# Transformer block kernel: first GELU product in fp16 parts, six norm applications on ScalarE and the bias addition moved in the full iterations

## What is computed

```python
x = x + _layernorm(_L0_attn_ref(_layernorm(x), rotation, entangle))      # softmax attention, 16 heads of 16
x = x + _layernorm(_L0_ffn_ref(_layernorm(x), W_r, W_k, W_v, mu_r, mu_k))  # r * (relu(k)^2 @ W_v), token shift
x = x + _layernorm(_L1_attn_ref(_layernorm(x), ...))                     # linear attention, then a GELU layer
x = x + _layernorm(_L1_ffn_ref(_layernorm(x), w_gate, w_up, w_down))     # gated layer with integer weights
# inside _L1_attn_ref, after the linear attention:
x2 = _layernorm(x, g2, be2)
h = jax.nn.gelu(x2 @ w1.T + b1, approximate=False)     # w1: 1024 x 256
x = x + (h @ w2.T + b2)
```

## Time and profile before

| | |
|---|---|
| median of 3 runs | 3242.41 us (3236.66 to 3253.96) |
| profiled execution | 3249.45 us, its span in the trace 3247.7 us |
| TensorE busy | 2945.7 us (91%) |
| ScalarE busy | 2332.9 us (72%), mostly before 2040 us |
| VectorE busy | 1478.6 us (46%), mostly after 2040 us |
| GpSimd busy | 217.9 us (7%) |

### The profile page before, as it was taken

The page is one execution under the profiler, slowest core; times in us unless marked ns, Lnnn a source line. Parts: engine busy times, 40 slices in busy tenths (PEclk is TensorE's granted clock), DMA queues, the critical chain, the costliest instruction groups (busy, mean ns, idle before and its releaser), DMA issues. The chain is left out here.

```text
span 3247.7 us, 48002 instructions
## 1 busy us (share of the span) xinstructions
PE 2945.7 (91%) x18048; PEld 1178.1 (36%) x18048; DVE 1478.6 (46%) x3536; ACT 2332.9 (72%) x2586; POOL 217.9 (7%) x193
## 2 busy tenths in 40 slices
PE   2998998999999999998999999389999999999996
PEld 0221221222222222222222222256666666666654
DVE  6221220422331332232411311568888888866574
ACT  2999999999999999998999999223343333333332
POOL 0000000000000000000000000111111111111110
PEclk9999999999999999999999999699999999999998
DMA  3411111311210211111111110222122111111010
GB/s 114 141 39 35 62 38 33 99 37 41 82 37 33 91 58 41 62 35 60 63 43 35 37 41 22 65 64 66 53 71 72 58 58 58 46 52 53 26 46 21
DMA packets 125602, 177.70 MB, mean 55 GB/s; under 512 B 42248, under 2 KB 100616, under 8 KB 125128
## 3 DMA queue, kind: packets, MB, share of 16 engines
q1 hardware_dynamic: 122392, 172.53, 16.4%
q10 hardware_dynamic: 2992, 2.23, 0.2%
HBM read 107.62 MB, written 67.11 MB: 54 GB/s over the span
## 5 line engine op out<-in xcount | busy, mean ns | idle before, releaser
L714 ACT ACTIVATE probs<-ps 128x1024 f32<-128x1024 f32 x2048 | 1895.1, 1172 | 102.3 <-PE ps L456 101.2
L582 PE MATMUL ps<-probs,vals 128*32 128x512 f32 x8192 | 1099.8, 610 | 0.0
L456 PE MATMUL ps<-qT,kT 64*128 64x512 f16 x4096 | 730.9, 387 | 109.2 <-DMA kT<-split_dram 26.9
L456 PEld LDWEIGHTS ps<-qT,kT 64*128 64x128 f16 x4096 | 173.0, 93 | 1152.6 <-ACT probs L714 1029.1
L869 DVE COPY sums<-ps 128x512 f32<-128x512 f32 x64 | 44.2, 691 | 529.5 <-PE ps L582 529.5
L582 PEld LDWEIGHTS ps<-probs,vals 128*32 128x32 f32 x8192 | 162.7, 108 | 298.8 <-issue 235.1
L1304 PE MATMUL layers_ps<-yT,weight_mem 128*128 128x512 f32 x512 | 227.5, 595 | 10.8 <-ACT hT L1543 10.8
L1310 PE MATMUL layers_ps<-weight_mem,hT 128*128 128x256 f32 x1024 | 231.5, 380 | 0.0
L1570 ACT ACTIVATE gate<-layers_ps 128x512 f32<-128x512 f32 x96 | 57.3, 597 | 226.4 <-PE layers_ps L1458 226.4
L1310 PEld LDWEIGHTS layers_ps<-weight_mem,hT 128*128 128x128 f32 x1024 | 193.0, 190 | 29.8
L1458 PE MATMUL layers_ps<-n4T,weight_mem 128*128 128x512 f16 x768 | 178.5, 387 | 7.3 <-DVE n4T L1793 7.3
(11 more groups left out here) (224 smaller groups left out, 2678.8 us busy)
## 6 DMA issues: line engine op xcount, KB each, us to landing
split_dram<-parts SPq DMA_DIRECT2D x28, 768.0 KB, 3.7
qT<-split_dram SPq DMA_DIRECT2D x126, 128.0 KB
kT<-split_dram SPq DMA_DIRECT2D x126, 128.0 KB
heads_dram<-result SPq DMA_DIRECT2D x64, 128.0 KB, 7.5
q_in<-q_dram SPq DMA_DIRECT2D x16, 512.0 KB, 3.3
n_in<-n_dram SPq DMA_DIRECT2D x16, 512.0 KB, 3.5
x_in<-x_dram SPq DMA_DIRECT2D x16, 512.0 KB, 5.3
out_dram<-y_out SPq DMA_DIRECT2D x16, 512.0 KB, 4.3
```

The source lines that it names most:

```text
L456: last = nc.tensor.matmul(SCORES[slot][:, n * BANK:(n + 1) * BANK], kT[buf][rows, j * P:(j + 1) * P], qT[buf][rows, q0:q0 + BANK], start=T ...
L582: mm = nc.tensor.matmul(ACC[32 * c:32 * c + 32, :], vals[buf][:, j, :], probs[:, j % PROBS, c * BANK:(c + 1) * BANK], start=(j == 0), stop ...
L714: nc.scalar.activation(probs[:, j % PROBS, half * T // 2:(half + 1) * T // 2], SCORES[slot_of(at)], ACT.Exp, scale=OPERAND_SCALE ** -2).th ...
```

## The change

1. **GELU product in fp16.** `w1` is scaled and split into a high and a low fp16 part, in place, once, on VectorE in head 59 of the attention stage (`parts_of_w1`, with `scales_of_w1` one head earlier, and one more absolute maximum over `w1` in head 57). `yT` is written as two fp16 parts as well: ScalarE copies the high part (scale `y_scale`, signal `yT_high`) and a new VectorE stage `y_low` makes the low part from PSUM and then signals `yT_done`. Each group of `fc` is now 6 fp16 matmuls of 512 columns in place of 2 float32 products, and the GELU has a scale from memory. This holds in all iterations.
2. **Norms.** GpSimd makes for six norms (attn, x1, f, x2, o, ffn) a second value, `shift = -mean * rstd`, and VectorE one more 128x4 instruction for `-mean`. In a new phase "full" (iterations 4 to 11) these six are applied by ScalarE, as `rstd * x + shift` (stages `ap_*`), and no longer by VectorE.
3. **Bias.** In the phase "full" the stage `b2` stands behind `in0` in the order of VectorE and GpSimd, where it stood behind `x4`.

```diff
+    "full": "ap_o fc0 ap_ffn mix fc1 uT mix_k mix_r nT keep up0 up1 high0 high1 ap_f up2 up3 high2 high3 ap_n2 up4 up5 high4 high5 ap_attn v k yT q keep_x1 ap_n1".split(),
...
-    "all": "ffn x4 b2 mix out n4 in0 n4_low f ... u y k_low o k_feat in1 q_low in2 q_feat kv diag".split(),
+    "all": "ffn x4 b2 mix out n4 in0 n4_low f ... u y k_low o k_feat y_low in1 q_low in2 q_feat kv diag".split(),
+    "full": "ffn x4_add mix out_add n4 in0 b2 n4_low f ... u y k_low o k_feat y_low in1_add q_low q_feat kv diag".split(),
...
+    if {"0", "1", "2", "b"} <= set(streams):
+        return "full"
...
                     pool.tensor_tensor(rstd[l][:, :], ve[l][:, :], neghalf[:, :], ALU.pow).then_inc(sem("rstd_" + l), 1)
+                    if l in shifted:
+                        pool.wait_ge(sem("rstd_" + l), 2 * c + 1)
+                        pool.tensor_tensor(shift[l][:, :], neg_mean[l][:, :], rstd[l][:, :], ALU.mult).then_inc(sem("rstd_" + l), 1)
...
-                        chan_out(ps[:, 6 + i % 2, :], W["w1"], i, yT).then_inc(sem("fc_mm"), 1)
+                        for n, (s, t) in enumerate(((0, 0), (1, 0), (0, 1))):
+                            for k in range(KC):
+                                last = nc.tensor.matmul(ps[:, 6 + i % 2, :], w1_16[:, s, k, i * P:(i + 1) * P], yT16[:, t, k, :],
+                                                        start=(n == k == 0), stop=(n == 2 and k == KC - 1))
+                        last.then_inc(sem("fc_mm"), 1)
...
-                A(yT[:, :, :], banks(0, 2), ACT.Copy).then_inc(sem("yT_done"), 1)
+                A(yT16[:, 0, :, :], banks(0, 2), ACT.Copy, scale=y_scale).then_inc(sem("yT_high"), 1)
...
-                        A(hT[:, i, :], ps[:, 6 + i % 2, :], ACT.Gelu, bias=W["b1"][:, 0, i:i + 1]).then_inc(sem("gelu_done"), 1)
+                        A(hT[:, i, :], ps[:, 6 + i % 2, :], ACT.Gelu, scale=fc_back, bias=W["b1"][:, 0, i:i + 1]).then_inc(sem("gelu_done"), 1)
...
+            def norm_apply(l, dst, src, c):
+                act.wait_ge(sem("rstd_" + l), 2 * c + 2)
+                for k in range(K4):
+                    ins = A(dst(k), src(k), ACT.Identity, scale=rstd[l][:, k:k + 1], bias=shift[l][:, k:k + 1])
+                return ins
...
+            def apply_ffn(c, past):
+                act.wait_ge(sem("stored"), c * 16)
+                norm_apply("ffn", blk(y_out), lambda k: blocks(4)[:, k, :], c).then_inc(sem("ffn_read"), 1)
...
+            def y_low(c, past):
+                dve.wait_ge(sem("yT_high"), c + 1)
+                V.scalar_tensor_tensor(yT16[:, 1, :, :].rearrange("p a n -> p (a n)"), wide(0, 2), y_scale, yT16[:, 0, :, :].rearrange("p a n -> p (a n)"),
+                                       ALU.mult, ALU.subtract).then_inc(sem("yT_done"), 1)
```

More of the change, by code:

```diff
@@ L1053, in second_half, with parts_of_w1 @@
+            def parts_of_w1():
+                ch = Chain(dve, weights_ready, W1_SCALED)
+                scaled, w1 = flat(xs[:, 0:KC * F1 // C, :]), flat(W["w1"])
+                high, low = (w1.bitcast(FP16)[:, s * KC * F1:(s + 1) * KC * F1] for s in range(2))
+                ch.link(V.tensor_scalar(scaled, w1, fc_scale[:, 1:2], None, ALU.mult))
+                ch.link(V.tensor_copy(high, scaled))
+                ch.link(V.tensor_tensor(low, scaled, high, ALU.subtract))
             def second_half(head, general):
@@ L1091, in _ @@
             second_half(NHD - 1, False)
-            dve.wait_ge(weights_ready, 3)
+            dve.wait_ge(weights_ready, W1_SCALED + 3)
 SHIFT = {"0": -EARLY, "1": 1 - EARLY, "2": 2 - EARLY, "l": LEAD, "m": LEAD + 1, "a": LEAD + 2, "b": LEAD + 3, "c": LEAD + 4}
 FIRST_CHUNK = {stream: EARLY if stream in "012" else 0 for stream in SHIFT}
-STAGES = {"0": "load_in in0 in1 in2 keep_x1", "1": "mix mix_r mix_k val f x2 n2 u", "2": "uT k k_low k_feat v q q_low q_feat kv", "l": "load_msg diag", "m": "msg y yT",
+STAGES = {"0": "load_in in0 ap_attn in1 in1_add in2 ap_n1 keep_x1", "1": "mix mix_r mix_k val f ap_f x2 x2_add n2 n2_eps ap_n2 u", "2": "uT k k_low k_feat v q q_low q_feat kv", "l": "load_msg diag", "m": "msg y yT y_low",
           "a": "load_x2 b2 fc0 fc1 proj0 proj1 proj2 proj3 o",
-          "b": "x4 n4 nT n4_low keep up0 up1 up2 up3 up4 up5 high0 high1 high2 high3 high4 high5 low0 low1 low2 low3 low4 low5 down0 down1 down2 down3",
-          "c": "ffn out"}
+          "b": "ap_o x4 x4_add n4 nT n4_low keep up0 up1 up2 up3 up4 up5 high0 high1 high2 high3 high4 high5 low0 low1 low2 low3 low4 low5 down0 down1 down2 down3",
+          "c": "ffn ap_ffn out out_add"}
 STREAM = {stage: stream for stream, stages in STAGES.items() for stage in stages.split()}
@@ L1112 @@
     "all": "fc0 mix fc1 uT mix_k mix_r nT val up0 up1 proj0 up2 up3 proj1 msg proj2 up4 up5 proj3 v k down0 yT down1 down2 q kv down3".split(),
+    "full": "fc0 mix fc1 uT mix_k mix_r nT val up0 up1 proj0 up2 up3 proj1 msg proj2 up4 up5 proj3 v k down0 yT down1 down2 q kv down3".split(),
     "drain": "fc0 fc1 nT proj0 up0 up1 proj1 up2 up3 proj2 msg proj3 up4 up5 down0 yT down1 down2 down3".split()}
@@ L1119 @@
     "fill": "mix k_low in0 k_feat q_low in1 q_feat f in2 x2 kv n2 u".split(),
-    "all": "ffn x4 b2 mix out n4 in0 n4_low f up0 up1 low0 low1 x2 up2 up3 low2 low3 msg n2 up4 up5 low4 low5 u y k_low o k_feat in1 q_low in2 q_feat kv diag".split(),
-    "drain": "x4 b2 ffn n4 out n4_low up0 up1 low0 low1 up2 up3 low2 low3 msg up4 up5 low4 low5 y o diag".split()}
+    "all": "ffn x4 b2 mix out n4 in0 n4_low f up0 up1 low0 low1 x2 up2 up3 low2 low3 msg n2 up4 up5 low4 low5 u y k_low o k_feat y_low in1 q_low in2 q_feat kv diag".split(),
+    "full": "ffn x4_add mix out_add n4 in0 b2 n4_low f up0 up1 low0 low1 x2_add up2 up3 low2 low3 msg n2_eps up4 up5 low4 low5 u y k_low o k_feat y_low in1_add q_low q_feat kv diag".split(),
+    "drain": "x4 b2 ffn n4 out n4_low up0 up1 low0 low1 up2 up3 low2 low3 msg up4 up5 low4 low5 y o y_low diag".split()}
 SP_ORDER = dict.fromkeys(PE_ORDER, "load_in load_msg load_x2 x2 n2 q_feat out".split())
 UNCOUNTED = [(name, count) for count, names in (
-    (1, "mix_mm k_mm val_mm uT_mm k2_mm v2_mm q_mm kv_mm n1T_done k_read x1_kept attn_normed x1_done carried f_done x2_step u_step kv_done"),
+    (1, "mix_mm k_mm val_mm uT_mm k2_mm v2_mm q_mm kv_mm n1T_done k_read x1_kept attn_normed x1_done carried f_done x2_step u_step kv_done rstd_attn rstd_x1 rstd_f rstd_x2"),
     (2, "stats_attn stats_x1 stats_f stats_x2 n2_step"),
@@ L1205, in later_layers @@
         rstd = {l: sb(f"rstd_{l}", [P, K4]) for l in norms}
+        shifted = ("attn", "x1", "f", "x2", "o", "ffn")
+        neg_mean, shift = ({l: sb(f"{n}_{l}", [P, K4]) for l in shifted} for n in ("neg_mean", "shift"))
         ve_n2, rstd_n2 = sb("ve_n2", [P, K4]), sb("rstd_n2", [P, K4])
```

88 lines of the change are left out of this document (73 added, 15 removed).

## The result

The changed kernel takes 3280.36 us (median of 4 runs, 3279.22 to 3281.32), the kernel before in the same comparison 3247.28 (4 runs, 3236.66 to 3253.96). The ratio is 1.0107 [1.0089, 1.0125]: slower, by 33 us. The forecast was 3264, set against a median of 3242.41, so slower by 21.6 us; 3280 lies inside the stated range of 3232 to 3284, near its far end. The profiled execution took 3279.22 us, its span is 3277.4; 29.7 us more than the span before.

A forecast was written before the change was run, and what follows sets the result against it. TensorE was taken to bound most of an iteration, but to wait at the seam between iterations for a chain on other engines. Terms 22 + 2 + 1 = +25 on 3249.45 gave 3274, lowered to 3264 us; range 3232 to 3284.

The forecast's parts named there:

- The wait of `q` for `y_low`: TensorE ahead of `q`: 2.4 us idle in every iteration with a `q`, which starts at K+6.95 instead of K+4.5.
- The wait inside `fc0`: TensorE ahead of the third group of `fc0`: stands still 3.8 us for the first GELU, ready at K+19.9.
- Wait for `xr`: TensorE ahead of `mix_k`: the wait shrinks to about 0.5 us.
- The norms on ScalarE: Four activations in a row on ScalarE take 2.0 us, bounds 1.6 and 2.3; three of six norms are in the chain.
- `b2` and `mix`: The bias addition cost `mix` 2.0 us; moved, `mix` starts at K+26.4 and takes 4.4 us, `mix_k` at K+31.0.
- Sum without slow stretches: Full iteration, K (VectorE's start of the `k` features) to next K: 31.0 + 44.5 = 75.5 us against 74.9.
- Rival (a): Full iterations: the same chain but no slow products after TensorE's waits, about 3244 us; chance 0.25.
- Slow stretches: Slower TensorE products after idle time: 1.2 us behind `q`'s wait, 1.3 in `fc0`; full iteration 78.0 us, +3.1.
- The other iterations: Iteration 3: -2 us; 12 and 13: +1.5 and +3.5; drain (15 to 18): -0.5 each; together +1.
- From 3274 to 3264: Final step: 3267 against the median of the runs, 7 us lower than the profiled one, then a little towards the 75.5.
- Rival (b): `fc0`: first GELU by K+16.1, so no wait there; `mix_k` at K+26, iteration 70.6 us, total 3200; chance 0.12.
- Rival (c): GpSimd's products hold up VectorE's addition or ffn's power before `mix`, each about 1 us an iteration: about 3275; chance 0.10.

The follow-up runs named there:

- The bias alone: Kernel before with only the bias addition `b2` moved behind `in0` in the full iterations: 3224.49 us, ratio 0.9928.
- both waits filled: Changed kernel with 15 unneeded fp16 products inside `fc0`'s wait and 10 more ahead of `q`: 3258.13 us, ratio 1.0023.
- `q` released: Changed kernel with ScalarE copying `yT` as float32 to SBUF, so `q` no longer waits for `y_low`: 3263.24 us, ratio 1.0056.
- the best version: Changed kernel, norm x1 back on VectorE, norm o earlier on ScalarE, norm ffn behind `n1T`'s copy, banks freed by ScalarE's `yT` copy: 3211.54 us, ratio 0.9895.
- norm o early: Changed kernel with ScalarE applying norm o ahead of the exponential of `q`, one iteration earlier: 3256.61 us, ratio 1.0026.
- `fc0`'s wait filled: Changed kernel with 15 unneeded fp16 products of 512 columns between the second and third group of `fc0`: 3263.54 us, ratio 1.0048.
- norms and bias: Changed kernel with the float32 product, float32 `yT` and no `y_low`: 3260.84 us, ratio 1.0038.

## Why the prediction was right or wrong

The direction and the chain were right: VectorE is no longer late, two norms ahead of the first GELU and one ahead of `n1T` are, and the moved bias pays only a part back. The signs named for the waits, the means of K to `mix_k` and of the period, and the activations came true. The size was wrong: 3264 is 16.4 us under the measured median, and only 16.7 of the 33.1 us by which that lies above the kernel before (3247.28). The step that failed is the last one, from the sum of 3274 down to 3264. By its steps:

- *The wait of `q` for `y_low`*: 2.4 forecast, 2.35 to 2.48 measured; VectorE's `q` instruction came at K+10.9 and not K+10.5. *The wait inside `fc0`*: 3.8 forecast, 3.69 to 3.79. *Wait for `xr`*: 0.5 forecast, 0.35.
- *The norms on ScalarE*: 2.0 us for four forecast, 2.06 measured; the 64 activations of norm x1 take 585 ns each in the mean, where 564 had been worked out. By "ScalarE: Activation LUTs" in the Trainium skill, section "What ACT_TABLE_LOAD costs", the prediction had estimated 2.1, and the trace agrees with the page. The GELU went from 687 to 780 ns, 0.09 as forecast.
- *`b2` and `mix`*: in iteration 8 the two `xk` instructions take 1.41 us, as forecast. The bias alone shortened the period by 2.5 us: 1.8 up to `mix_k`, and the rest the slow `mix_k`, which the prediction had counted too (0.8).
- *Sum without slow stretches*: K to mix_k 31.0 forecast, 31.2 in the run with both waits filled; period 75.5 forecast, 75.7 measured. Rival (a) was this chain at 3244; with both waits filled the time was 3258, with slow stretches left only outside the full iterations.
- *Slow stretches*: mis-sized, though little. Forecast 2.5 us an iteration (1.2 behind `q`'s wait, 1.3 in `fc0`), measured 33.9 - 31.2 = 2.7. The split was off: `q` was slow in 3 of 7, 0.7 us on average, not in 7 of 10; the third group was slow every time, by 1.3 to 2.55 us, 1.9 on average. Over the seven iterations the change cost +24.2 where +22 was forecast.
- *The other iterations*: +3 forecast behind iteration 11, +4.3 measured; without the wait of `q` for `y_low` the end would be 8 us shorter, by the run with `q` released. From K of iteration 11 to `up0` of iteration 14 it is +7.0, where +5 had been forecast for iterations 12 and 13. In the drain the forecast was -0.5 an iteration; `up0` of iteration 14 to `up0` of iteration 18 is 206.55 us against 206.9, -0.1 each, and -2.2 from there to the end. `up0` came 1.0 to 3.2 us earlier against `fc0` in iterations 15 to 18 (1.4 forecast), but in iterations 14 and 16 it took 5.30 us instead of 3.62, after 2.1 us of idle time. Up to the end of iteration 4: 0 forecast, +1.1 measured: +0.4 up to the end of iteration 2 (the preparation of `w1` lies ahead of it), -1.9 in iteration 3 (-2 forecast) and +2.6 in iteration 4 (+2 forecast). With the term above the sum was +25, 3274 against the profiled execution, and +29.7 was measured: 4.8 us of the miss.
- *From 3274 to 3264*, the other 11.6 us, and the step that failed: the 7 us between the profiled execution (3249.45) and the median of three runs (3242.41) of the kernel before were taken off the changed kernel too, and 3 more "towards the 75.5". Those 7 us were an accident of three runs. The 48 runs of the kernel before beside the experiments have a median of 3250.1 and 43 of them are longer than 3242.41; the profiled execution is an ordinary one. The changed kernel showed no such difference: its four runs lie within 2.1 us, and its median is 1.1 us above its profiled execution. And what was shaded by 3 us was the price of the slow stretches, which was if anything too low.
- *Rival (b)* did not come true, but its mechanism is the best version's: with the first GELU at K+14.7 `mix_k` comes at K+26.1, where (b) had 26. *Rival (c)*: the GpSimd product takes 0.20 us in 78 of 80 cases; the power for ffn took 1.91 to 2.01 us in iterations 5 to 11, where it had mostly taken 1.04, off the chain in the changed kernel. It is in the chain where norm ffn waited 1.39 us for it, above.

What stays open: why the runs of some of these kernels vary by 2 us and those of others by 17. In the kernel before the time goes with the granted clock of the run: 0.976 to 0.980 in the ten of the 48 runs under 3245 us, 0.973 or 0.974 in the 19 above 3251. A mix of slow and ordinary products from run to run would fit that, but is not shown by a trace of a short run; and the kernel with both waits filled has no slow product in the full iterations of its trace and still varies between 3252.08 and 3260.66. Nor do the traces say what makes one product slow and the next, after the same wait, ordinary.

## What to carry to other kernels

Work that is moved to an engine with much idle time is free only in the gap where it fits: ScalarE had 8.9 us free ahead of `q`'s exponential. Behind that exponential the norm o cost 2 us an iteration and the slow products after the longer wait, 24 us in all; inside the gap it did not delay the exponential (K+12.2 with and without it, where `q` is ordinary). A shorter product gives nothing where TensorE already waits; take the wait away first, then shorten. Price a long wait on TensorE (here 2 us and more) with the slow product that may follow it. And a median of three runs of a kernel that spreads over 17 us is no base to correct a forecast by: compare with more runs, or trace with trace.

## What the runs showed of the hardware

- Products without use in the waits made the kernel 22 us faster; the granted clock of the full iterations went from 0.96 to 1.00.
- After 2.35 to 2.48 us of idle time `q` took 3.67 or 5.37 us in the changed kernel, slow in 3 of 7 iterations. With norm o early (2.35 to 2.70 us) it was slow in 6 of 7, with `fc0`'s wait filled in 2 of 7, though the third group was slow in neither of these two; so what the third group did before is not the whole rule. The third group was slow in 7 of 7 after 3.69 to 3.79 us, in 6 of 7 after 3.50 to 3.62 (norms and bias), in none of 7 after 1.72 to 1.82 (norm o early).
- GpSimd's 128x4 power takes 1.01 us alone and took 1.91 to 2.01 us, in each of iterations 5 to 11 of the changed kernel, when VectorE's addition of two SBUF operands had started 0.1 to 0.2 us ahead of it (here at 2526.59, 1.22 us, shown above):

```profile
2526.70 1.98 POOL L1317 TENSOR_TENSOR rstd_ffn<-ve_ffn,neghalf_k 128x4 f32<-128x4 f32 x1 [7.42 <-DVE ve_ffn L1712]
2528.75 0.20 POOL L1320 TENSOR_TENSOR shift_ffn<-neg_mean_ffn,rstd_ffn 128x4 f32<-128x4 f32 x1
```

"SBUF — State Buffer" in the Trainium skill, section "Who interferes with whom", says that such a VectorE instruction and a GpSimd instruction that reads SBUF block each other; the trace agrees, and here it is the GpSimd side that pays.
